# Score banks of the cross-attention in turns, hidden units rounded by ScalarE, and the self-attention's output weights rounded by ScalarE

## The chip, the cores and the metric

One NeuronCore of one Trainium2 chip runs the whole kernel in one launch. The metric is the device time of one execution in microseconds (us), taken as the median of the runs shown. Everything is computed in float32 accuracy: each operand of a large matmul is split into a rounded part ("hi") and a rest ("lo"), and three products (hi x hi, hi x lo, lo x hi) are summed in PSUM.

## The reference, cut to what matters

```python
# layer 0: cross-attention on 64 context rows, 16 heads of 16, then an MLP
q = layernorm(x, ln1) @ Wq ; k, v = split(layernorm(ctx, ln2) @ Wkv)
x = x + softmax(q k^T * 0.25) v @ Wproj + bproj
x = x + gelu(layernorm(x, ln3) @ W1 + b1) @ W2 + b2
# layer 1: self-attention on 512 rows, 16 heads of 64
n = layernorm(x, g1)
x = x + softmax((n @ Wq1)(n @ Wk1)^T * 0.125) (n @ Wv1) @ Wo1 + bo1
# then cross-attention (Wq2, Wk2, Wv2, Wo2) and a gated MLP (Wp, Wf)
```

x is (8, 512, 256), the context (8, 64, 192), the hidden width of layer 0 is 1024, the inner width of layer 1 is 1024, and Wo1 is 1024 x 256.

## The kernel before, in words

The program has four stretches: products of the context with layer 1's weights, layer 0 (the loop called loop0), layer 1's self-attention (loop3), and layer 1's cross-attention with the gated MLP (loop4). Each engine has its own function for each stretch, with the order of its work written out by hand; the engines meet through semaphores. An engine does its instructions strictly in the written order, so a wait holds up all that stands behind it.

**Layer 0's loop** has 44 iterations. Iteration i of i = 0 to 31 computes the attention scores of one piece c = i of 128 rows (16 heads x 64 keys, so 128 x 1024 numbers in two PSUM banks). A batch b is four pieces. In one iteration of the attention part the engines do the following.

- TensorE (`pe_attention0`): it turns the first half of piece i-2 (four transposes, L778), computes the scores of piece i (six matmuls), and turns the second half of piece i-2. In the middle of an iteration stand `query(b)` in iterations i = 3, 7, ... (12 matmuls of 512 columns), the attention's `output` in odd iterations (24 matmuls of 256 columns) and its `project` in even ones (12 matmuls). A layernorm's transpose (`ln_transpose`, eight at L152) stands in even iterations, for the attention's input (kind "x", i % 4 == 2) or for the MLP's (kind "g", i % 4 == 0).
- VectorE (`dve_attention0`): the largest score of each row and head (L1008), the difference to it (L1014), the sum and reciprocal of the exponents (L1001, L1004), the rests of what was turned (L162), residual additions (L1071, L1045), the statistics of the next layernorm (L239, L243, L246) and its shift (L276).
- ScalarE (`act_attention0`): the exponent (L947, with a table load), the "hi" copies (L156), the layernorm's scale (4 x 128x256) and affine step (2 x 128x512), and the MLP's GELU (L916, with a table load).
- GpSimd (`pool_attention0`): it divides the exponents (L1098), splits the layernorm's output (L159, L165), computes 1/sqrt(variance) (L256), and adds the bias to x (L1136).

The scores of every piece lie in PSUM banks 0 and 1, as do a query's projection and a layernorm's transposes. So `scores(c)` waits until `differences(c - 1)` has read the banks (semaphore `sc0_sub`), and `query` and `ln_transpose` wait in the same way.

From iteration 10 (LAG0) on, the MLP runs beside the attention, ten iterations behind: two hidden units n = 2(i - 10) and n + 1 (of 64, each 128 x 512) per iteration. Their up-projections go to bank 4, their down-projections add up in banks 6 and 7, which are thus empty in iterations 0 to 9. A hidden unit goes from `up` (TensorE) to GELU (ScalarE, into hf1), `rounds` (the "hi" part), `rests` (VectorE, the "lo" part) and `down` (TensorE). GpSimd does `rounds` for the first 48 units (iterations 10 to 33), ScalarE for the last 16:

```python
NPOOL = 2 * (N0 + 2 - LAG0)          # L683: 48
...
if NPOOL <= n < NM:                  # L943, ScalarE
    rounds(n)
```

TensorE does `down(n - 2)` after `up(n)`, and `down(n - 1)` at the end of the iteration.

**Layer 1's self-attention** has one unit s per pair of heads and batch, 64 in all, each in four parts j. Its output weights Wo1 are eight jobs of 128 x 256 (list `g4`). A job is a DMA (L353) into one of two staging halves, a rounding to "hi", and a rest to "lo": by GpSimd for jobs 0, 3 and 6, by VectorE for the others. A half can be loaded again once the job two before it has its rest (`sp_weight`). Before, VectorE rounds and takes rests of two jobs in each part of unit 0 (`dve_weight`, L357 and L162, called at L1603 to L1605). The first use of these weights, and of the staging halves as work space, is in part 3 of unit 1.

## Time and profile before

| | |
|---|---|
| median of 3 runs | 2342.82 us (2341.16 to 2347.05) |
| the profiled execution, own time | 2332.97 us |
| its span in the profile | 2331.2 us |
| TensorE busy | 2135.2 us, 92% |
| VectorE busy | 1627.0 us, 70% |
| ScalarE busy | 1449.5 us, 62% |
| GpSimd busy | 1104.8 us, 47% |
| mean granted TensorE clock | 0.97 of full |
| layer 0's loop | 112.8 to about 600 us |
| self-attention, unit 0 / unit 1 | from 612.2 / from 634.4 us |

A row of the timeline gives the start in us from the span's start, the duration, the engine, the line (a helper's line for most copies, rests and matmuls), the operation, output and input, and in brackets how long the engine had been idle and what released it. PE is TensorE, DVE is VectorE, ACT is ScalarE, POOL is GpSimd; PS is PSUM, R and F are SBUF areas, F for float32 and R for split operands. Engine times overlap, so a busy time says nothing of the end by itself; what counts is which engine waits for which at each place.

### The profile page before, as it was taken

To read this page: it belongs to the slowest core of one execution; us is meant where nothing else is said; L and a number is where in the kernel's file an instruction comes from. 1 tells how busy PE (TensorE), PEld (TensorE's weight loads), DVE (VectorE), ACT (ScalarE), POOL (GpSimd) and SP (SyncE) were. 2 spreads that over 40 slices of the span, in tenths; PEclk is the share of its full clock that TensorE was granted. 3 is DMA by queue.
4 is the path that set the end of the run, shared out by engine and by line. 5 is a ranking of instruction groups with operands and counts; after the bars stand their busy time and mean duration, and the time that the engine had idled before them with its cause. 6 is when DMAs were issued, how large, how long until landed. Compare 5 with 4: busy or idle time off the path is not lost. (4 is left out here: it accounts for less than half of the span.)

```text
span 2331.2 us, 31301 instructions
## 1 busy us (share of the span) xinstructions
PE 2135.2 (92%) x11628; PEld 1780.3 (76%) x11628; DVE 1627.0 (70%) x2353; ACT 1449.5 (62%) x2098; POOL 1104.8 (47%) x867
## 2 busy tenths in 40 slices
PE   6867999997799999999999999999998799999998
PEld 4655778786577787777777777777876689889987
DVE  6566667664578777787777878778776866666553
ACT  5444666654477777777777777777775354545431
POOL 2145455543145444454454544545444675566432
PEclk8968999999999999999999999999999999999999
DMA  7710000011000000100001000010013411111000
GB/s 237 264 41 5 21 21 21 10 48 46 28 24 15 24 24 15 37 15 24 24 14 33 18 23 26 15 33 15 17 37 130 162 46 55 55 55 46 10 10 19
DMA packets 84280, 102.67 MB, mean 44 GB/s; under 512 B 29664, under 2 KB 61152, under 8 KB 83616
## 3 DMA queue, kind: packets, MB, share of 16 engines
q1 hardware_dynamic: 84128, 100.66, 12.9%
q8 instruction: 93, 1.52, 0.3%
q14 instruction: 59, 0.48, 0.1%
HBM read 65.50 MB, written 33.82 MB: 43 GB/s over the span
## 5 line engine op out<-in xcount | busy, mean ns | idle before, releaser
L146 PE MATMUL PS<-R 128*128 128x512 f32 (+1 forms) x2944 | 1028.6, 349 | 98.9 <-DVE R L162 55.9
L147 PE MATMUL PS<-R 128*128 128x512 f32 (+1 forms) x2944 | 999.2, 339 | 0.0
L148 PE MATMUL PS<-R 128*128 128x512 f32 (+1 forms) x2944 | 998.9, 339 | 0.0
L146 PEld LDWEIGHTS PS<-R 128*128 128x128 f32 x2944 | 567.4, 193 | 213.3 <-DVE R L162 70.2
L156 ACT ACTIVATE R<-PS 64x512 fp32r<-64x512 f32 (+4 forms) x860 | 460.3, 548 | 275.6 <-PE PS L1768 129.4
L148 PEld LDWEIGHTS PS<-R 128*128 128x128 f32 x2944 | 567.0, 193 | 61.1
L147 PEld LDWEIGHTS PS<-R 128*128 128x128 f32 x2944 | 568.3, 193 | 54.9
L162 DVE TENSOR_TENSOR R<-F,R 128x1024 fp32r<-128x1024 f32 (+2 forms) x416 | 478.6, 1156 | 44.1 <-ACT R L156 22.3
L159 POOL TENSOR_SCALAR R<-F 128x512 fp32r<-128x512 f32 (+1 forms) x343 | 294.8, 862 | 347.2 <-DVE F L1921 147.0
L1463 ACT ACTIVATE F<-PS 128x1024 f32<-128x1024 f32 x256 | 262.9, 1027 | 177.5 <-DVE R L162 122.3
L159 POOL TENSOR_SCALAR R<-R 64x512 fp32r<-64x512 f32 x128 | 143.0, 1131 | 391.4 <-ACT R L156 391.4
L1549 DVE TENSOR_REDUCE F<-PS 128x2 f32<-128x1024 f32 x256 | 301.4, 1215 | 16.2 <-PE PS L1349 16.2
L162 DVE TENSOR_TENSOR R<-PS,R 128x512 fp32r<-128x512 f32 (+3 forms) x348 | 181.4, 542 | 187.5 <-ACT R L156 187.1
L165 POOL TENSOR_TENSOR R<-F,R 128x512 fp32r<-128x512 f32 (+2 forms) x126 | 233.7, 1857 | 35.7 <-ACT R L156 19.1
L1530 DVE TENSOR_TENSOR R<-PS,R 64x512 fp32r<-64x512 f32 x128 | 88.0, 688 | 221.9 <-ACT R L156 221.9
L156 ACT ACTIVATE R<-F 128x1024 fp32r<-128x1024 f32 (+2 forms) x190 | 167.0, 896 | 55.5 <-PE PS L148 54.1
L156 ACT ACTIVATE F<-PS 64x512 f32<-64x512 f32 (+3 forms) x280 | 160.1, 593 | 44.6 <-PE PS L148 37.8
L1349 PE MATMUL PS<-R 128*128 128x512 f32 x512 | 164.2, 402 | 8.6 <-ACT F L156 4.9
L1315 PE MATMUL PS<-R 128*128 128x512 f32 x512 | 163.1, 400 | 7.9 <-ACT R L156 7.3
L1311 PE MATMUL PS<-R 128*128 128x512 f32 x512 | 166.7, 407 | 1.9 <-ACT F L1463 1.9
L152 PE MATMUL PS<-F 128*128 128x128 f32 x592 | 89.6, 289 | 54.0 <-DVE F L1549 30.0
L1659 POOL TENSOR_TENSOR F<-F 128x512 f32<-128x512 f32 x64 | 83.4, 1302 | 116.0 <-DMA F<-sd 116.0
(90 smaller groups left out, 1983.5 us busy)
## 6 DMA issues: line engine op xcount, KB each, us to landing
F<-sd SPq DMA_DIRECT2D x128, 128.0 KB, 2.8
xs<-F SPq DMA_DIRECT2D x16, 512.0 KB, 2.6
F<-xs SPq DMA_DIRECT2D x16, 512.0 KB, 3.6
gd<-F SPq DMA_DIRECT2D x8, 768.0 KB, 3.5
vd<-F SPq DMA_DIRECT2D x8, 768.0 KB, 5.7
R<-gd SPq DMA_DIRECT2D x6, 1024.0 KB, 5.6
R<-vd SPq DMA_DIRECT2D x6, 1024.0 KB, 5.6
F<-in_x SPq DMA_DIRECT2D x8, 512.0 KB, 4.9
```

The source lines that it names most:

```text
L146: nc.tensor.matmul(o, L[0], Rr[0], start=start, stop=False, skip_group_check=share)
L147: nc.tensor.matmul(o, L[0], Rr[1], start=False, stop=False, skip_group_check=share)
L148: return nc.tensor.matmul(o, L[1], Rr[0], start=False, stop=stop, skip_group_check=share)
L156: return nc.scalar.activation(o, i, ACT.Identity, **k)
L159: return nc.gpsimd.tensor_scalar(o, i, 1.0, 1.0, ALU.mult, ALU.mult)
L162: return nc.vector.tensor_tensor(o, i, f32(hi), ALU.subtract)
L165: return nc.gpsimd.tensor_tensor(o, i, f32(hi), ALU.subtract)
L1311: nc.tensor.matmul(bank(h), ka[i][h][:, kk], qa[i][h], start=True, stop=False)
L1315: m = nc.tensor.matmul(bank(h), kb[i][h][:, kk], qb[i][h], start=False, stop=True)
L1349: m = nc.tensor.matmul(bank(b0 + h), qa[i][h][:, 128 * q:128 * q + 128], ka[i][h], start=True, stop=True)
L1463: nc.scalar.activation(pst3[n % 2], bank(0, 2), ACT.Exp, scale=0.125).then_inc(e3.sem, 1)
L1549: nc.vector.tensor_reduce(M3[:, q, 0:128:64], bank(b0, 2).rearrange("p (a b) -> p a b", a=2), AX.X, ALU.max).then_inc(b3_max.sem, 1)
```

## The change

It has three parts.

1. In iterations 0 to 9 of layer 0's loop, odd pieces have their scores in banks 6 and 7, even ones in banks 0 and 1. `scores(c)` then waits for `differences(c - 2)`. The layernorms' transposes of these iterations (i = 2, 6, 8) go to banks 6 and 7 and wait for `differences(i - 1)` in place of `differences(i)`. `query(1)` and `query(2)`, in banks 0 and 1, wait for the differences of pieces 2 and 6 in place of 3 and 7.
2. `rounds` is done by ScalarE for all 64 hidden units. GpSimd's 48 go away. The two events become one.
3. Wo1's jobs are rounded by ScalarE: one job in each part of unit 0 (jobs 0 to 3), and two in each of the parts 0 and 1 of unit 1 (jobs 4 to 7). The rests stay with the engines that had them, at the new places. SyncE's loads follow: job i + 2 is asked for where job i is handled.

```diff
@@ -679,9 +679,7 @@
         av0_mm, o0_hi, o0_lo = event("d_mm", 2 * NB), event("o_hi", 2 * NB), event("o_lo", 2 * NB)
         o0_mm, o0_add = event("o_mm", 2 * NB), event("x_add", 2 * NB)
         up_mm, gelu, h_lo, down_mm = [event(n, NM) for n in ("up_mm", "gelu", "h_lo", "down_mm")]
-
-        NPOOL = 2 * (N0 + 2 - LAG0)
-        h_hi, h_act = event("h_hi", NPOOL), event("h_act", NM - NPOOL)
+        h_hi = event("h_hi", NM)
         res = event("res", 2 * NB)
 
 
@@ -696,6 +694,14 @@
         norm0_at = {"x": (0, P_LN1W, P_LN1B), "g": (0, P_LN3W, P_LN3B), "s": (2, P_G1, P_B1)}
 
         turn_bank = (2, 5)
+
+        def score_bank(c):
+
+            return 6 if c < LAG0 and c % 2 == 1 else 0
+
+        def norm0_bank(i):
+            return 6 if i < LAG0 else 0
+
         first1 = (N0 + 7, N0 + 8, N0 + 9, N0 + 11)
 
         def norm0_to(kind, b):
@@ -755,7 +761,7 @@
             def query(b):
                 pe.wait_ge(ln_nl, number0["x", b])
                 wait_weights(pe, "q")
-                pe.wait_ge(sc0_sub, 4 * b - 1)
+                pe.wait_ge(sc0_sub, 4 * b - 2 if 4 * b - 1 < LAG0 else 4 * b - 1)
                 for g in range(2):
                     for k in range(2):
                         m = mm3(bank(g), [v[:, k, 128 * g:128 * g + 128] for v in W0q], [v[:, k, :] for v in ns[b % 2]],
@@ -782,11 +788,11 @@
                 b, q = divmod(c, 4)
                 pe.wait_ge(q0_lo, 2 * b + 1)
                 pe.wait_ge(k0_in[b % 2], b // 2)
-                pe.wait_ge(sc0_sub, c - 1)
+                pe.wait_ge(sc0_sub, c - 2 if c <= LAG0 else c - 1)
                 if c - 1 in norm0:
                     pe.wait_ge(ln_aff, 2 * norm0[c - 1][2] + 1)
                 for g in range(2):
-                    m = mm3(bank(g), [v[:, g, 128 * q:128 * q + 128] for v in Q1], [kd_b[b % 2][:, hl, g, :] for hl in range(2)],
+                    m = mm3(bank(score_bank(c) + g), [v[:, g, 128 * q:128 * q + 128] for v in Q1], [kd_b[b % 2][:, hl, g, :] for hl in range(2)],
                             True, True)
                 m.then_inc(sc0_mm.sem, 1)
 
@@ -863,8 +869,8 @@
                 if i % 2 == 0 and ok((i - 4) // 2, 2 * NB):
                     project((i - 4) // 2)
                 if i in norm0:
-                    pe.wait_ge(sc0_sub, min(i, N0 - 1))
-                    ln_transpose(norm0[i][2], 0)
+                    pe.wait_ge(sc0_sub, i - 1 if i < LAG0 else min(i, N0 - 1))
+                    ln_transpose(norm0[i][2], norm0_bank(i))
                 if ok(n + 1, NM):
                     up(n + 1)
                 if i % 4 == 2 and ok((i - 2) // 4, NB) and i > 2:
@@ -919,7 +925,7 @@
             def rounds(n):
                 act.wait_ge(gelu, n)
                 act.wait_ge(down_mm, n - 3)
-                act_copy(h1[n % 3][0], hf1[n % 3]).then_inc(h_act.sem, 1)
+                act_copy(h1[n % 3][0], hf1[n % 3]).then_inc(h_hi.sem, 1)
 
             act.wait_ge(g5_mm, 15)
             for job in g1:
@@ -940,7 +946,7 @@
                     act_weight(job)
                 if ok(n, NM):
                     gelus(n)
-                if NPOOL <= n < NM:
+                if ok(n, NM):
                     rounds(n)
                 if ok(i, N0):
                     act.wait_ge(sc0_sub, i)
@@ -949,13 +955,13 @@
                     query(i // 4 + 1)
                 if i in norm0:
                     kind, b, k = norm0[i]
-                    ln_affine(k, norm0_at[kind][1], norm0_at[kind][2], 0)
+                    ln_affine(k, norm0_at[kind][1], norm0_at[kind][2], norm0_bank(i))
                 if i + 1 in norm0:
                     kind, b, k = norm0[i + 1]
                     ln_scale_act(k, xbuf(norm0_at[kind][0], b))
                 if ok(n + 1, NM):
                     gelus(n + 1)
-                if NPOOL <= n < NM:
+                if ok(n + 1, NM):
                     rounds(n + 1)
                 if i % 2 == 1 and ok((i - 3) // 2, 2 * NB):
                     m_ = (i - 3) // 2
@@ -1005,20 +1011,17 @@
 
             def largest(c):
                 dve.wait_ge(sc0_mm, c)
-                nc.vector.tensor_reduce(mx4, heads(bank(0, 2)), AX.X, ALU.max).then_inc(sc0_max.sem, 1)
+                nc.vector.tensor_reduce(mx4, heads(bank(score_bank(c), 2)), AX.X, ALU.max).then_inc(sc0_max.sem, 1)
 
             def differences(c):
                 dve.wait_ge(sc0_max, c)
                 dve.wait_ge(w_lo_pool, [j.rest for j in g1 if j.by_pool][-1])
                 dve.wait_ge(t0_mm, 2 * (c - 3) + 1)
-                nc.vector.tensor_tensor(heads(E1[c % 3]), heads(bank(0, 2)), mx4.unsqueeze(2).to_broadcast([128, 16, 64]),
+                nc.vector.tensor_tensor(heads(E1[c % 3]), heads(bank(score_bank(c), 2)), mx4.unsqueeze(2).to_broadcast([128, 16, 64]),
                                         ALU.subtract).then_inc(sc0_sub.sem, 1)
 
             def rests(n):
-                if n < NPOOL:
-                    dve.wait_ge(h_hi, n)
-                else:
-                    dve.wait_ge(h_act, n - NPOOL)
+                dve.wait_ge(h_hi, n)
                 dve_rest(h1[n % 3][1], hf1[n % 3], h1[n % 3][0]).then_inc(h_lo.sem, 1)
 
             for job in g1:
@@ -1087,11 +1090,6 @@
                     next(ahead)
 
         def pool_attention0(ahead):
-            def rounds(n):
-                pool.wait_ge(gelu, n)
-                pool.wait_ge(down_mm, n - 3)
-                pool_copy(h1[n % 3][0], hf1[n % 3]).then_inc(h_hi.sem, 1)
-
             def divided(c):
                 pool.wait_ge(rec0, c)
                 ev = E1[c % 3].rearrange("p (h s) -> p h s", h=16)
@@ -1116,12 +1114,8 @@
                     divided(i - 1)
                 for job in weights0_at(i):
                     pool_weight(job)
-                if ok(n, NPOOL):
-                    rounds(n)
                 if LAG0 <= i - 1 < N0:
                     divided(i - 1)
-                if ok(n + 1, NPOOL):
-                    rounds(n + 1)
                 if i in norm0:
                     kind, b, k = norm0[i]
                     if kind == "g":
@@ -1249,6 +1243,12 @@
 
         def v3_bank(u):
             return 6 if u else 5
+
+        def weights3_at(s, j):
+
+            if s == 0:
+                return g4[j:j + 1]
+            return g4[2 * j + 4:2 * j + 6] if s == 1 and j < 2 else []
 
         def sp_attention1():
             sp.wait_ge(x_out[x_at(0, 7)], store_no[0, 7])
@@ -1276,9 +1276,8 @@
                     e = s - 3
                     if j == 1 and ok(e, N3) and e % 8 == 7:
                         sp_store(2, e // 8, xs, o3_add, e)
-                    if s == 0:
-                        sp_weight(g4, 2 * j + 2)
-                        sp_weight(g4, 2 * j + 3)
+                    for job in weights3_at(s, j):
+                        sp_weight(g4, g4.index(job) + 2)
                     at = tail3(s, j)
                     if at == 0:
                         sp.wait_ge(qk_mm, 2 * N3 - 1)
@@ -1491,6 +1490,8 @@
                         project_k(u)
                     if ok(u, N3) and u > 0 and j == 1:
                         value(u)
+                    for job in weights3_at(s, j):
+                        act_weight(job)
                     if ok(t, N3) and j in (1, 2):
                         rounded(t, j)
                     if ok(d, N3) and j == 3:
@@ -1600,9 +1601,8 @@
                             rests(4 * s + 2)
                     if ok(u, N3) and j in (1, 2):
                         largest(u, 2 * j - 2, 2)
-                    if s == 0:
-                        for job in g4[2 * j:2 * j + 2]:
-                            dve_weight(job)
+                    for job in weights3_at(s, j):
+                        dve_weight_rest(job)
                     for _ in range(early4.get(tail3(s, j), 0)):
                         next(ahead)
                     if more and j == 3 and p == 4:
@@ -1666,9 +1666,8 @@
                         pool.wait_ge(e3, 4 * t + j)
                         pool.wait_ge(d3_mm, 4 * (t - 1) + j)
                         pool_copy(P3[0][:, j, :], pst3[j % 2]).then_inc(p3_pool.sem, 1)
-                    if s == 0:
-                        for job in g4[2 * j:2 * j + 2]:
-                            pool_weight(job)
+                    for job in weights3_at(s, j):
+                        pool_weight(job)
                     for _ in range(early4_pool.get(tail3(s, j), 0)):
                         next(ahead)
                     if j == 2 and more and p == 6:
```

Three places show how the instructions of the engines move. The first is TensorE in iterations 1 and 2 of layer 0's loop: the second half of the scores of piece 0, the scores of piece 1 (six matmuls), the four transposes of piece 0 (waiting for `p_mul`, GpSimd's division), and the first matmul of the scores of piece 2. Before:

```order
L147 MATMUL PS<-R,R1 128x512
L148 MATMUL PS<-R,R1 128x512
L146 MATMUL PS<-R,R1 128x512 [waits sc_sub]
L147 MATMUL PS<-R,R1 128x512
L148 MATMUL PS<-R,R1 128x512
L146 MATMUL PS<-R,R1 128x512
L147 MATMUL PS<-R,R1 128x512
L148 MATMUL PS<-R,R1 128x512
L778 MATMUL PS<-F,F1 128x128 [waits p_mul]
L778 MATMUL PS<-F,F1 128x128 x3
L146 MATMUL PS<-R,R1 128x512 [waits sc_sub]
```

And now:

```order
L147 MATMUL PS<-R,R1 128x512
L148 MATMUL PS<-R,R1 128x512
L146 MATMUL PS<-R,R1 128x512
L147 MATMUL PS<-R,R1 128x512
L148 MATMUL PS<-R,R1 128x512
L146 MATMUL PS<-R,R1 128x512
L147 MATMUL PS<-R,R1 128x512
L148 MATMUL PS<-R,R1 128x512
L784 MATMUL PS<-F,F1 128x128 [waits p_mul]
L784 MATMUL PS<-F,F1 128x128 x3
L146 MATMUL PS<-R,R1 128x512 [waits sc_sub]
```

The order is the same; piece 1 has no wait for VectorE any more.

The second place is ScalarE in layer 0's loop where the MLP runs beside the attention: from the GELU of the second unit of an odd iteration on, over the whole of the following even one (i % 4 == 0). R1<-F1 128x512 is a rounding. Before:

```order
L916 ACTIVATE F<-PS,F 128x512 [waits up_mm]
L156 ACTIVATE R<-PS 128x512 [waits o_mm,d_mm]
L156 ACTIVATE R<-PS 128x4x128 [waits t_mm] x2
L916 ACTIVATE F<-PS,F 128x512 [waits h_lo,up_mm]
L947 ACT_TABLE_LOAD
L947 ACTIVATE F<-F 128x1024 [waits sc_sub]
L156 ACTIVATE F<-PS,F 128x512 [waits ln_tr]
L156 ACTIVATE F<-PS,F 128x512
L916 ACT_TABLE_LOAD [waits h_lo]
L916 ACTIVATE F<-PS,F 128x512 [waits up_mm]
```

And now:

```order
L922 ACTIVATE F1<-PS,F 128x512 [waits up_mm]
L156 ACTIVATE R1<-F1 128x512 [waits down_mm,gelu]
L156 ACTIVATE R1<-PS 128x512 [waits o_mm,d_mm]
L156 ACTIVATE R1<-PS 128x4x128 [waits t_mm] x2
L922 ACTIVATE F1<-PS,F 128x512 [waits h_lo,up_mm]
L156 ACTIVATE R1<-F1 128x512 [waits down_mm,gelu]
L953 ACT_TABLE_LOAD
L953 ACTIVATE F1<-F1 128x1024 [waits sc_sub]
L156 ACTIVATE F<-PS,F 128x512 [waits ln_tr]
L156 ACTIVATE F<-PS,F 128x512
L922 ACT_TABLE_LOAD [waits h_lo]
L922 ACTIVATE F1<-PS,F 128x512 [waits up_mm]
```

One rounding stands ahead of the exponent and its table load, the other ahead of the attention output's copy and of the two turned halves. The number of table loads is the same, 96 in the program.

The third place is ScalarE in the first parts of unit 1 of the self-attention, now; before, the four rows R<-F3 128x256 weren't there:

```order
L1462 ACTIVATE F3<-PS 128x1024 [waits p_lo,c_mm]
L156 ACTIVATE R3<-PS 64x512 x2
L156 ACTIVATE R3<-PS 64x512 [waits qk_mm]
L156 ACTIVATE R3<-PS 64x512
L156 ACTIVATE R<-F3 128x256 [waits w_in0]
L156 ACTIVATE R<-F3 128x256 [waits w_in1]
L1462 ACTIVATE F3<-PS 128x1024 [waits p_lo,c_mm]
L156 ACTIVATE R3<-PS 128x4x64 [waits v_set,v_mm]
L156 ACTIVATE R3<-PS 128x4x64
L156 ACTIVATE R<-F3 128x256 [waits w_in0]
L156 ACTIVATE R<-F3 128x256 [waits w_in1]
L156 ACTIVATE R3<-F3 128x1024 [waits d_mm,exp]
```

Jobs 4 and 5 stand ahead of the exponent of part 1 (L1463 before), jobs 6 and 7 behind the value's copies and ahead of the rounding of the exponents of part 1. Both pairs wait for their DMA (`w_in0`, `w_in1`).

## Rows read from the trace of the kernel before

**Rows 1.** Windows by stage: us, busy of PE, PEld, DVE, ACT, POOL, granted clock, DMA.
```profile
112.80:214.10 101.30, 69.75 (x328) 58.09 (x329) 65.74 (x113) 43.44 (x75) 49.13 (x35) 0.71 0.09 26
...
241.50:296.40 54.90, 49.90 (x308) 43.22 (x306) 37.48 (x65) 34.12 (x49) 27.68 (x20) 0.94 0.07 23
...
404.30:456.90 52.60, 47.09 (x308) 41.14 (x307) 37.40 (x65) 34.05 (x49) 27.68 (x20) 1.00 0.03 11
...
612.20:634.40 22.20, 13.77 (x51) 10.21 (x52) 16.82 (x26) 11.41 (x17) 5.49 (x7) 0.85 0.12 37
634.40:651.50 17.10, 16.03 (x76) 12.48 (x75) 12.70 (x14) 13.71 (x20) 4.28 (x4) 1.00 0.00 0
```

**Rows 2.** Timeline, PE, waits in iterations 2, 3, 6 and 7 of layer 0.
```profile
128.90 1.97 PE L152 MATMUL PS<-F 128*128 128x128 f32 x8 [3.33 <-DVE F L1014]
...
138.82 0.77 PE L146 MATMUL PS<-R 128*128 128x512 f32 x1 [2.63 <-DVE F L1014]
...
171.11 1.70 PE L152 MATMUL PS<-F 128*128 128x128 f32 x8 [2.54 <-DVE F L1014]
...
183.35 0.77 PE L146 MATMUL PS<-R 128*128 128x512 f32 x1 [6.36 <-DVE F L1014]
```

**Rows 3.** Timeline, DVE and ACT, iterations 3 and 7 of layer 0.
```profile
147.73 0.69 DVE L162 TENSOR_TENSOR R<-PS,R 128x512 fp32r<-128x512 f32 x1 [2.10 <-ACT R L156]
...
189.26 2.07 ACT L156 ACTIVATE F<-F 128x256 f32<-128x256 f32 x4
...
192.21 0.69 DVE L162 TENSOR_TENSOR R<-PS,R 128x512 fp32r<-128x512 f32 x1 [2.12 <-ACT R L156]
```

**Rows 4.** Timeline, PE, waits in iterations 25 to 27 of layer 0.
```profile
421.58 0.39 PE L146 MATMUL PS<-R 128*128 128x256 f32 x1 [0.64 <-DVE R L162]
428.29 0.39 PE L146 MATMUL PS<-R 128*128 128x256 f32 x1 [1.07 <-DVE R L162]
442.44 0.39 PE L146 MATMUL PS<-R 128*128 128x256 f32 x1 [2.39 <-DVE R L162]
...
445.47 0.47 PE L146 MATMUL PS<-R 128*128 128x512 f32 x1 [1.33 <-DVE F L1014]
```

**Rows 5.** Timeline, DVE, iterations 24 to 27 of layer 0.
```profile
411.51 0.17 DVE L246 TENSOR_SCALAR F<-F 128x4 f32<-128x4 f32 x1
...
417.86 0.58 DVE L276 SCALAR_TENSOR_TENSOR F<-F 128x4 f32<-128x4 f32 x1 [1.54 <-POOL F L256]
...
426.35 1.88 DVE L162 TENSOR_TENSOR R<-F,R 128x512 fp32r<-128x512 f32 x1
...
432.43 0.63 DVE L162 TENSOR_TENSOR R<-F,R 128x512 fp32r<-128x512 f32 x1
...
436.37 0.71 DVE L162 TENSOR_TENSOR R<-PS,R 64x64 fp32r<-64x64 f32 x4 [2.71 <-ACT R L156]
...
438.96 1.04 DVE L246 TENSOR_SCALAR F<-F 128x4 f32<-128x4 f32 x1
```

**Rows 6.** Timeline, POOL, iterations 25 and 26 of layer 0.
```profile
414.13 2.71 POOL L165 TENSOR_TENSOR R<-F,R 128x1024 fp32r<-128x1024 f32 x1
...
425.29 2.40 POOL L1136 TENSOR_TENSOR F<-F 128x1024 f32<-128x1024 f32 x1
...
437.58 2.40 POOL L165 TENSOR_TENSOR R<-F,R 128x1024 fp32r<-128x1024 f32 x1
```

**Rows 7.** Timeline, ACT, a GELU and ScalarE's own rounding behind it, late in layer 0.
```profile
581.65 0.69 ACT L916 ACTIVATE F<-PS,F 128x512 f32<-128x512 f32 x1
582.37 0.63 ACT L156 ACTIVATE R<-F 128x512 fp32r<-128x512 f32 x1
```

**Rows 8.** Line L357 (the roundings of Wo1) and the loads of Wo1, L353.
```profile
L357 DVE CAST R<-F x8: 275/282/885, 616.6 to 630.4; 128x256 fp32r<-128x256 f32 x8
...
DMA to landing us min/median/max: 2.0/2.0/2.3
```

**Rows 9.** Timeline, PE, last part of unit 0 of the self-attention.
```profile
629.18 1.11 PE L152 MATMUL PS<-F 128*128 128x128 f32 x4 [3.87 <-DVE F L1549]
```

## The prediction

> **What bounds the kernel now.** I read the windows by stage first, then TensorE's waits in the timeline, then the engine that ended each. Over the whole span TensorE is busy 92%, so what can be won lies in the stretches where it stands still. The first ten iterations of layer 0's loop take 101.3 us with TensorE busy 69.8 us at a granted clock of 0.71, so much of even that is time at 1.2 GHz; no engine is full there, it is a chain that goes round [rows 1]. With the MLP beside the attention, four iterations take 52.6 us at full clock, TensorE 47.1 busy, ScalarE 34.05, VectorE 37.4, GpSimd 27.7; the same four take 54.9 us where the clock is 0.94 [rows 1]. Unit 0 of the self-attention takes 22.2 us against 17.1 for unit 1, with VectorE busy 16.8 us in it [rows 1]. The change touches these three stretches and nothing else.
>
> **Part 1, score banks in turns (iterations 0 to 9).** It adds no instruction. It takes away waits for VectorE's difference L1014: 3.33 us before the transposes of iteration 2, 2.63 before the query of iteration 3, 2.54 before the transposes of iteration 6, 6.36 before the query of iteration 7 [rows 2]. That is 14.9 us of TensorE's standstill, but it counts only as far as VectorE's own chain then moves. I follow it with the trace's durations.
>
> - Iteration 2: the transposes start 3.3 us earlier, but ScalarE still does its affine step behind the exponent of piece 2. That step starts 1.0 us earlier, and so do the scores of piece 3, GpSimd's split and the end of iteration 3's difference.
> - Iteration 3: the query needs GpSimd's split (ready about 135.0) and the transposes of piece 1, which end about 135.2. It starts there in place of 138.82, 3.6 us earlier. The query's copies, the output's 24 matmuls and the output's rest on VectorE, now at 147.73 behind 2.10 us of idle time [rows 3], all come 3.6 us earlier. Everything VectorE does in iteration 4 stands behind that rest. Gain 3.6 us.
> - Iterations 4 and 5: VectorE is never idle before its scores arrive, and iteration 5's output waits for VectorE's rest of a turned half. Gain 0.
> - Iteration 6: the transposes no longer wait, but `value(1)` behind them needs the residual addition, and ScalarE the exponent. The value copies and VectorE's rests of them come 0.65 us earlier.
> - Iteration 7: the query can start at 177.3 in place of 183.35 [rows 2]. What then comes last is ScalarE: the exponent of piece 7, two query copies, the four layernorm scales of 2.07 us, and only then the output's copy. VectorE's rest of it moves from 192.21 [rows 3] to about 187.55. That is 4.66 us, of which 0.65 was counted: 4.0.
> - Iterations 8 and 9: ScalarE's affine step is in order behind the exponent. Gain 0.1.
>
> Sum 8.35 us. The bounds are 0, if ScalarE's and VectorE's order holds all of it back, and 14.9 us, the waits themselves. I take 8.4: the one number comes from following both queues.
>
> **Part 2, ScalarE rounds all hidden units (iterations 10 to 33).** 48 roundings leave GpSimd and come to ScalarE. There one lasts 0.63 us and starts 0.72 us behind the GELU's start [rows 7]; with the overlap that is lost before it I count 0.67 us in its queue, 5.4 us per four iterations, so ScalarE goes from 34.05 to about 39.4 of 52.6 us. No table load is added. TensorE waits four times in four iterations: 0.64, 1.07, 2.39 and 1.33 us [rows 4].
>
> - Iteration 25, 0.64 us. VectorE was late because its layernorm shift waited 1.54 us for GpSimd's L256 [rows 5], which stood behind the split L165 of 2.71 us [rows 6], which stood behind the second rounding. Without it the split starts at 410.4 in place of 412.4, L256 ends about 414.9, and VectorE's difference comes 1.8 us earlier. The wait goes.
> - Iteration 26, 1.07 us. VectorE's rest of a hidden unit took 1.88 us, where its like takes 0.63 [rows 5], while GpSimd's bias addition L1136 ran (425.29 to 427.69, [rows 6]). That addition stood behind a rounding that waited for the GELU; now it follows the division and is over by about 423.6. ScalarE's rounding delays the turned half by 0.67 us, less what iteration 25 gave. The rest then ends about 426.1, when TensorE arrives (426.2). The wait goes, narrowly.
> - Iteration 27, 2.39 and 1.33 us. Here the chain runs through ScalarE: affine step, table load, GELU, and now the rounding (+0.67), then the value copies for which VectorE is already waiting 2.71 us. On VectorE the small L246 took 1.04 us, while GpSimd's split ran; the split is now earlier, and L246 alone takes 0.17 us [rows 5, 6]: -0.87. Net 0.2 us per wait chain. What is late next is the same chain.
>
> Three times 0.64, four times 1.07 (the first two such waits come at 265.6 and 320.4), six times 0.2, and 0.6 us for the last iterations, where the waits are smaller: 1.9 + 4.3 + 1.2 + 0.6 = 8.0 us. The bounds: all 5.4 us of waits in six rounds of four iterations gone (a gain of 32), or each of 48 roundings in the chain (a loss of 32). I take 8, since the rows name what ended each wait.
>
> What the lock is worth: by durations alone the rest in iteration 26 would come 0.67 us later through ScalarE and keep its 1.88 us. The rows show 1.88 against 0.63 whenever a GpSimd addition of two SBUF operands runs beside it. The Trainium skill (SBUF — State Buffer, "SBUF: two separate sides") says that a VectorE instruction with two SBUF inputs and a GpSimd one that reads SBUF take a shared port pair as an exclusive lock for the whole instruction. By that rule it matters only that they don't meet, and the 4.3 us come; if the stretching had another cause, part 2 would give 8.0 - 4.3 = 3.7 us.
>
> **Part 3, Wo1's roundings.** VectorE loses eight of 0.28 to 0.5 us, 2.7 us in all [rows 8], and the rests of jobs 4, 5 and 7, 2.4 us, leave unit 0. ScalarE gains eight, estimated at 0.36 us, between VectorE's 0.28 and the 0.63 of twice the columns on ScalarE [rows 7, 8]. In unit 0 VectorE is the chain, but in part 0 its next work waits for ScalarE's value copies, so 0.95 us comes there, 0.3 in part 1 and 1.6 in parts 2 and 3: the transposes that wait 3.87 us at 629.18 [rows 9] come 2.85 us earlier. Unit 1 pays. Job 6 can be loaded only when VectorE has job 4's rest, now at about 640.3 (on the old scale); the DMA takes 2.0 us [rows 8], so ScalarE stands at job 6 until about 642.4, and the rounding of part 1's exponents, the exponent of part 2 and job 7 stand behind it. That rounding comes 3.1 us later; behind it VectorE has its own work (three more rests) and ends 1.1 us later. Net 2.85 - 1.1 = 1.75, I take 1.7. Bounds: +2.85, and -3.1 if unit 0 gives nothing and the stall isn't absorbed.
>
> **Sum:** 8.4 + 8.0 + 1.7 = 18.1 us. The span becomes 2331.2 - 18.1 = 2313.1, that execution's time 2332.97 - 18.1 = 2314.9. The profiled execution was 9.85 us below the median of the runs shown, so on their scale I forecast 2342.8 - 18.1 = 2324.7, say **2325 us**.
>
> **Rivals.**
>
> - *The banks bring nothing.* TensorE's queries come earlier, but ScalarE's order (exponent, query copies, scales) and VectorE's hold the chain. For it: those engines also idle only for one another in iterations 4 and 5. Against it: iteration 3's output has nothing of ScalarE's before it but two copies. Time 2325 + 8.4 = 2333. The Trainium skill (TensorE: Matmul & The Clock Gate, "HAM oscillation") tells of a kernel where double-buffering PSUM "gave no further gain"; that would be this rival. Rows 2 show the wait that it removes here, so I hold it less likely.
> - *The clock adds to it.* Four iterations take 2.3 us less at full clock than at 0.94 [rows 1], and the first ten iterations ran at 0.71, where 69.75 busy us would be 20 fewer at full clock, most of them off the chain. With fewer standstills three rounds (6.9 us) and an estimated tenth of those 20 could be won: 2325 - 9, about 2316.
> - *Wo1 loses.* The stall at job 6 isn't absorbed and unit 0 gives nothing: 2325 + 1.7 + 3.1 = 2330.
> - *ScalarE becomes the chain; slower.* Place: the second rounding of each iteration, ahead of the attention output's copy, the turned halves and the value copies. It decides if ScalarE's idle time at these places is less than the 1.3 us that an iteration adds. Then 48 x 0.67 = 32.2 us are on the path, part 2's 8.0 fall away, and 10.1 remain: 2342.8 + 32.2 - 10.1 = 2365. With one of two roundings on the path it is 2342.8 + 16.1 - 10.1 = 2349. Against it: ScalarE idles (52.6 - 34.05) / 4 = 4.6 us per iteration. For it: VectorE waits for ScalarE in iteration 27 already.
>
> **How the numbers follow.** My forecast has 0.50, the clock's case 0.20, the banks' 0.12, Wo1's 0.10, ScalarE's 0.08 (0.05 of it at 2349 or above). 0.3% is 7 us, about what a measurement of this kernel tells from no change: faster is below 2335.8. Faster: the forecast, the clock and Wo1 (0.80) less 0.04 for a smaller gain than worked out, and half of 0.12, whose time lies 3 us from the border: 0.82. Slower 0.05, same 0.13. The range reaches from 2311, the clock's case with the banks' upper bound half reached, to 2337, the banks' case with Wo1's loss: 2311 to 2337.
>
> **What would show it.** Right: the first ten iterations take about 93 us in place of 101.3; TensorE has no wait for VectorE's difference before the queries of iterations 3 and 7; four iterations with the MLP take 50.5 us at full clock, the waits of 0.64 and 1.07 are gone and one of about 2.2 is left; unit 0 takes 19.4 us and unit 1 18.2, with a ScalarE wait for a DMA. Wrong: a wait of TensorE for rests longer than 2.4 us, or VectorE idle for ScalarE over more than before in iterations 10 to 33.

## The result, and the profile after

The changed kernel takes 2314.57 us (median of 4 runs, 2312.75 to 2317.42), the kernel before beside it 2341.99 us. The ratio is 0.988, 95% interval [0.986, 0.990]. Run once more in a later comparison it gave 2317.71 us and 0.989 [0.987, 0.991], against 2339.53 for the kernel before beside it. The forecast was 2325: the time lies in its range, but the gain is 27.4 us the first time and 21.8 the second, where 18.1 were summed.

Page of the profile after, busy time of each engine:

```profile
PE 2127.5 (92%) x11628; PEld 1774.7 (77%) x11628; DVE 1610.2 (70%) x2345; ACT 1482.0 (64%) x2154; POOL 1070.6 (46%) x819
```

ScalarE has 32.5 us more than before (48 roundings of 0.63 and the output weights), GpSimd 34.2 less, VectorE 16.8 less, and TensorE 7.7 less for the same 11628 matmuls. Some 5 to 6 of these 7.7 lie in the first ten iterations (69.75 us busy before; 64.79 after, 63.49 from the first mark on), where the granted clock went from 0.71 to 0.83.

Windows by stage after, the stretches of [rows 1] (us, busy of PE, PEld, DVE, ACT, POOL, granted clock, DMA): ten iterations (from 1.3 us ahead of the first mark on; from the mark they are 89.6 us), four iterations twice, unit 0, unit 1.

```profile
117.70:208.60 90.90, 64.79 (x339) 53.72 (x338) 66.01 (x112) 42.82 (x76) 49.20 (x35) 0.83 0.10 29
235.40:285.70 50.30, 46.76 (x307) 41.34 (x307) 34.15 (x65) 39.19 (x56) 22.45 (x12) 1.00 0.07 25
336.10:388.40 52.30, 49.56 (x307) 43.50 (x306) 34.19 (x65) 39.14 (x56) 22.45 (x12) 0.93 0.07 23
593.10:612.10 19.00, 13.25 (x48) 10.16 (x49) 11.84 (x14) 12.62 (x22) 4.80 (x6) 0.82 0.10 28
612.10:631.30 19.20, 17.22 (x78) 12.90 (x78) 14.98 (x18) 15.03 (x25) 4.71 (x5) 1.00 0.05 14
```

I cut every trace at the same marks: VectorE's maximum of each piece of scores (the first of them is called the first mark), and in the self-attention the start of a unit's first exponent on ScalarE. All times in us; "rounds" are the four times four iterations from piece 12 on, "last" is pieces 28 to 31.

| | 0 to 10 | 10 to 12 | rounds | last | unit 0 | unit 1 |
|---|---|---|---|---|---|---|
| before | 101.3 | 27.5 | 54.9, 54.8, 53.1, 52.7 | 33.3 | 22.2 | 17.2 |
| after | 89.6 | 26.8 | 50.3, 50.3, 52.4, 50.3 | 34.5 | 19.0 | 19.2 |
| after, again | 89.2 | 27.1 | 52.4, 50.4, 50.7, 52.4 | 34.5 | 19.0 | 19.3 |

The profiled spans differ by only 20.2 us (2331.2 and 2311.0). Six of the missing us lie ahead of the first mark, in code that the change doesn't touch: it came at 112.8 us before and at 119.0 after, and in the twelve other traces at 115.1 to 120.1. From that mark to unit 2 the two traces differ by 26.5 us, close to the medians' 27.4; the second trace of the changed kernel differs by 22.9, with 21.8 between its medians. Of the 26.5 us, 2.0 lie between piece 31 and unit 0, where the kernels with that stretch unchanged scatter by as much (119.9 to 121.9 us).

TensorE after, from the timeline: around the query of iteration 3, where [rows 2] had 2.63 us of waiting, and the two waits that are left in a round, where [rows 4] had four.

```profile
140.69 0.48 PE L784 MATMUL PS<-F 128*128 128x128 f32 x2
141.13 0.50 PE L146 MATMUL PS<-R 128*128 128x512 f32 x1
141.46 0.39 PE L147 MATMUL PS<-R 128*128 128x512 f32 x1
141.69 0.40 PE L148 MATMUL PS<-R 128*128 128x512 f32 x1
...
143.99 0.29 PE L146 MATMUL PS<-R 128*128 128x256 f32 x1
...
424.79 0.39 PE L146 MATMUL PS<-R 128*128 128x256 f32 x1 [2.19 <-DVE R L162]
427.81 0.47 PE L146 MATMUL PS<-R 128*128 128x512 f32 x1 [1.33 <-DVE F L1020]
```

The query starts 22.1 us behind the first mark in place of 26.0, with no wait. From its second matmul on they follow each other at 0.23 us. In the kernel before, same view and query, they came at 0.43; the last row is the first matmul of the output behind it:

```profile
139.39 0.63 PE L147 MATMUL PS<-R 128*128 128x512 f32 x1
139.82 0.63 PE L148 MATMUL PS<-R 128*128 128x512 f32 x1
...
144.08 0.32 PE L146 MATMUL PS<-R 128*128 128x256 f32 x1
```

Those are the two levels of the clock, 2.4 GHz after and 1.2 GHz before. From the query's start to the output's it takes 2.86 us after and 5.26 before. ScalarE in unit 1 after, timeline: it stands for the transfer of job 6 and, shortly, of job 7.

```profile
620.46 0.42 ACT L156 ACTIVATE R<-F 128x256 fp32r<-128x256 f32 x1 [2.35 <-DMA F<-in_w_o]
621.15 1.37 ACT L156 ACTIVATE R<-F 128x256 fp32r<-128x256 f32 x2 [0.27 <-DMA F<-in_w_o]
```

### The profile page after: what moved, and what is told of

It reads as the page before. It is cut to its first block and busy times, and to the rows that moved or that the text cites. A ratio compares the mean times of both kernels' runs of the same rounds, so it can differ in the third digit from the quotient of the medians.

```text
span 2311.0 us, 31301 instructions
## 1 busy us (share of the span) xinstructions
PE 2127.5 (92%) x11628; PEld 1774.7 (77%) x11628; DVE 1610.2 (70%) x2345; ACT 1482.0 (64%) x2154; POOL 1070.6 (46%) x819
## 5 line engine op out<-in xcount | busy, mean ns | idle before, releaser
L162 DVE TENSOR_TENSOR R<-F,R 128x1024 fp32r<-128x1024 f32 (+2 forms) x416 | 465.9, 1125 | 44.0 <-ACT R L156 22.2
L159 POOL TENSOR_SCALAR R<-F 128x1024 fp32r<-128x1024 f32 (+1 forms) x295 | 265.6, 902 | 281.9 <-DVE F L1920 147.1
L156 ACT ACTIVATE R<-F 128x1024 fp32r<-128x1024 f32 (+2 forms) x246 | 200.2, 828 | 60.0 <-PE PS L148 54.8
L1096 POOL TENSOR_TENSOR F<-F 128x1024 f32<-128x1024 f32 x32 | 67.9, 2123 | 167.1 <-DVE F L1010 167.1
L1659 POOL TENSOR_TENSOR F<-F 128x512 f32<-128x512 f32 x64 | 82.6, 1290 | 120.9 <-DMA F<-sd 120.9
```

The lines of the kernel that those rows point to most:

```text
L156: return nc.scalar.activation(o, i, ACT.Identity, **k)
L159: return nc.gpsimd.tensor_scalar(o, i, 1.0, 1.0, ALU.mult, ALU.mult)
L162: return nc.vector.tensor_tensor(o, i, f32(hi), ALU.subtract)
```

## The experiments

Theory: the three parts do what the forecast worked out, and TensorE's clock adds to each, since fewer and shorter standstills leave it high for longer. Rival: the steps themselves were undersized, and the clock only went along.

### Each part alone

Each is the kernel before with one part's lines of the diff.

> The kernel before with part 1 alone (score banks in turns, with the early query and transposes); nothing else is changed. Theory A (my steps, at the clock of the trace of before): the first ten iterations take 93 us, the kernel gains 8.4 us. Theory B (the steps plus the clock: TensorE stands still less just before iteration 3's query, so that its 12 matmuls run at 2.4 GHz): the first ten iterations take 89 to 90 us, iteration 3 to 4 gains 4.8 us and not 3, the kernel gains about 12 us. Rival (the banks bring nothing by themselves): within 2 us of before. Stretches after iteration 10 as before in all of them.

> The kernel before with part 2 alone (ScalarE rounds all hidden units). First ten iterations as before, 101 us. Theory A (steps): four iterations at full clock take 50.4 us in place of 52.6, the kernel gains 8 us. Theory B (steps plus clock): the rounds that were at 0.94 take 50.4 us too, or 52.3 where the clock still falls, the kernel gains 11 to 13 us. Rival (it is only ScalarE that got longer): slower by some us, a wait for rests over 2.4 us.

> The kernel before with part 3 alone (ScalarE rounds Wo1). Theory: unit 0 takes 19.0 us in place of 22.2, unit 1 takes 19.2 in place of 17.2, with ScalarE waiting about 2.4 us for the load of job 6; net 1.2 us faster, within the noise of the timing. Rival: the stall isn't absorbed later, net slower by 1 us or more.

| | median | ratio, interval | 0 to 10 | 10 to 12 | rounds | last | unit 0 | unit 1 |
|---|---|---|---|---|---|---|---|---|
| banks | 2327.26 | 0.9945 [0.9933, 0.9957] | 89.8 | 28.4 | 55.0, 54.8, 54.7, 53.1 | 33.3 | 22.2 | 17.2 |
| rounding | 2328.59 | 0.9953 [0.9941, 0.9965] | 100.5 | 26.8 | 50.5, 52.5, 50.4, 50.6 | 34.5 | 22.2 | 17.2 |
| Wo1 | 2335.56 | 0.9987 [0.9977, 0.9996] | 100.6 | 27.5 | 54.9, 54.8, 54.7, 53.0 | 33.3 | 18.8 | 19.1 |

The kernel before in this comparison: 2339.24 us. Each part moves its own stretch; the banks alone also give back 0.9 us between pieces 10 and 12. The gains are 12.0, 10.7 and 3.7 us by the medians, 26.3 in all, beside 27.4 and 21.8 for the changed kernel: as far as the scatter lets one see, the parts add up. The banks came out as theory B said. The rounding's 10.7 lies between A's 8 and B's 11 to 13. Wo1 has 1.5 us on the marks (1.2 expected), which the interval of its ratio takes in. Where a kernel leaves the first ten iterations as they were, they take 100.5 to 101.4 us.

### The query's wait put back

```diff
 # the changed kernel, query(b)
-pe.wait_ge(sc0_sub, 4 * b - 2 if 4 * b - 1 < LAG0 else 4 * b - 1)
+pe.wait_ge(sc0_sub, 4 * b - 1)
```

> The changed kernel, but the query of a block waits again for the differences of the chunk just before it, as in the kernel before, while the scores' banks still alternate. Forecast's reading (the first wait of iterations 3 and 7, about 3.3 and the larger part of 6.4 us, is ended by the query's own wait, so that letting it go early is most of the first part's gain): ten iterations grow from 89.6 to 93 to 97 us, the kernel to 2318 to 2322 (ratio 0.990 to 0.992). Rival (the scores, whose wait was loosened as well, carry the gain and the query would be waited for little): ten iterations 90 to 91 us, within 1.5 us of the changed kernel, ratio 0.988 to 0.989.

2320.53 us, ratio 0.9934 [0.9915, 0.9953]; ten iterations 97.8 us. Timeline, TensorE, the queries of iterations 3 and 7:

```profile
142.97 0.77 PE L146 MATMUL PS<-R 128*128 128x512 f32 x1 [2.63 <-DVE F L1020]
...
185.16 0.77 PE L146 MATMUL PS<-R 128*128 128x512 f32 x1 [6.89 <-DVE F L1020]
```

The two queries' waits alone give back 8.2 of the 11.7 us that ten iterations had gained. The forecast's reading holds, and ten iterations came out even a little above its band. The other 3.5 us stay with the alternating scores and transposes.

### The clock alone

Products that nothing uses, put where TensorE stands idle ahead of these two queries. Every wait of the kernel before stays.

```diff
 # the kernel before, TensorE's loop; fill(k, b) is k matmuls of 128x512 into bank b
+if i in (3, 7):
+    fill({3: 4, 7: 12}[i], 6)
 if i % 4 == 3 and ok(i // 4 + 1, NB):
     query(i // 4 + 1)
```

> The kernel before, with products that nothing uses added on TensorE: 4 of 128x512 ahead of iteration 3's query and 12 ahead of iteration 7's, into a bank that is empty there, where TensorE idles on a wait anyway. Nothing else moves, and no wait is taken away. Theory (the first ten iterations lose time to the clock after each long wait of TensorE, and the part of the change's gain that was not forecast is this clock): the granted clock of the first ten iterations rises from 0.71 to 0.77 or more, the query of iteration 3 and what follows it runs at the short spacing, ten iterations take 98 to 100 us instead of 101.3, and the kernel 2336 to 2338 us against 2339.2 (ratio 0.998 to 0.999). Rival (the clock does not answer to such products, or the waits of the ramp swallow what it gives): ten iterations within 0.5 us of 101.3, ratio 1.000; if the added products delay the query by more than the clock gives, up to 1.0015.

2329.68 us against 2338.04, ratio 0.9963 [0.9950, 0.9976]: more work, and a faster kernel. Timeline, TensorE, the query of iteration 3, and the window of ten iterations:

```profile
141.15 0.47 PE L146 MATMUL PS<-R 128*128 128x512 f32 x1 [1.32 <-DVE F L1020]
141.46 0.40 PE L147 MATMUL PS<-R 128*128 128x512 f32 x1
```

```profile
115.10:213.00 97.90, 69.51 (x345) 57.92 (x346) 65.87 (x113) 43.59 (x75) 49.24 (x35) 0.79 0.09 27
```

The query starts at the same place, 26.04 us behind the first mark in both kernels. Its matmuls now run at full clock, from its start to the output's it takes 2.84 us in place of 5.26, and the first four iterations take 35.1 us in place of 37.5: 2.4 us from the clock alone. (In three other traces with these iterations unchanged they took 36.7 to 37.7; in one of them the query's first five matmuls came at full clock too.) The ten iterations win 3.4 us against the trace of before, 2.7 against the shortest of the others. The median won 8.4, more than the added products' own stretch shows; what lies behind the other 5 us I can't tell from one trace.

### The lock between VectorE and GpSimd

Two kernels move GpSimd's bias addition: in the kernel before it goes ahead of the second rounding; in the changed kernel it is held back until ScalarE's second rounding.

```diff
 # the kernel before, pool loop: the addition of bias to xbuf moved up
+<the addition, L1136>
 if ok(n + 1, NPOOL):
     rounds(n + 1)
-<the addition, L1136>
 # the changed kernel, ahead of the addition
+if ok(n + 1, NM) and i < N0:
+    pool.wait_ge(h_hi, n + 1)
```

> The kernel before, with GpSimd's bias addition ahead of its second rounding in odd iterations of layer 0; all roundings stay with GpSimd. Theory (the addition at the wrong moment stretches VectorE's rest in iteration 26 and its like): the rest takes 0.63 us again, TensorE's waits of 1.07 us go, those of 0.64 and 2.39 stay, 4 us faster. But the rounding now waits up to 0.7 us for the addition where the GELU is ready before it, so a little may be lost. Rival (what helps is that ScalarE rounds, not the order): rests as long as before or the second rounding late, no gain.

> The changed kernel, but in the first layer's loop GpSimd's bias addition (2.40 us) additionally waits until ScalarE has rounded the second unit of hidden products of that iteration, so that it falls again on VectorE's rest of those products. Theory (GpSimd's bias addition running beside VectorE's subtraction stretches that subtraction from 0.63 us to about 1.9, and this is what the PE waits of 0.64 and 1.07 us in a four-iteration round were made of): a rest of 1.5 to 1.9 us is back wherever the addition stands, once or twice in four iterations, the four-iteration round grows from 50.4 to 51.5 to 52.5 us, over the four rounds and the ramp 5 to 9 us in all, so 2319 to 2324 us against 2314.6 of the changed kernel (ratio to the kernel before 0.992). Rival (the gain of the second part is ScalarE's earlier rounding alone, and GpSimd's place does not matter): within 0.1% of the changed kernel, ratio to the kernel before 0.988 to 0.989, rounds still 50.4.

Addition moved up: 2330.55 us, ratio 0.9970 [0.9956, 0.9983], rounds 51.4, 51.4, 51.4 and 53.9; of the four waits of [rows 4] the one of 1.07 us is gone and 0.64 and 2.39 are as before. At full clock a round is 1.2 us shorter; the 8.7 us by the medians are twice the 4 expected, and part of it is that the clock fell in one of the four rounds, in place of three of four. Addition held back: 2306.88 us against 2338.04, rounds 51.1, 51.2, 51.2 and 51.2. Its ratio of 0.988 [0.986, 0.990] is what the rival said, not the 0.992 of the theory: the 0.8 us a round, some 3 in all, don't stand out of the scatter of a whole run, and only the marks show them. Timeline, GpSimd and VectorE, iteration 26: first the kernel with the addition moved up, then the one with it held back (there in iteration 26 too).

```profile
420.19 2.38 POOL L1127 TENSOR_TENSOR F<-F 128x1024 f32<-128x1024 f32 x1
...
423.31 0.68 DVE L162 TENSOR_TENSOR R<-F,R 128x512 fp32r<-128x512 f32 x1
```

```profile
407.32 2.40 POOL L1132 TENSOR_TENSOR F<-F 128x1024 f32<-128x1024 f32 x1 [2.10 <-ACT R L156]
...
407.76 1.29 DVE L162 TENSOR_TENSOR R<-PS,R 128x512 fp32r<-128x512 f32 x2 [4.30 <-ACT R L156]
408.96 1.31 DVE L162 TENSOR_TENSOR R<-F,R 128x512 fp32r<-128x512 f32 x1
```

The rest with two SBUF operands takes 0.68 us when the addition is over, 1.31 when it meets its last 0.8 us, and took 1.88 when it met its last 1.3 [rows 5, 6]. In both cases where they meet it ends 0.54 to 0.55 us behind the addition (410.27 and 409.72; 428.23 and 427.69), however early it started: I read that as standing until the addition was over, and then running. The two rests just ahead of it have one operand in PSUM and took 1.29 us with the addition beside them. That is the rule of the Trainium skill (SBUF — State Buffer, "SBUF: two separate sides"), and the trace agrees down to PSUM operands being free of it. I had expected 1.5 to 1.9 us and rounds of 51.5 to 52.5: ScalarE's rounding ends early enough that the two meet only at the end, so the stretch costs 0.8 us a round in place of 1.1 to 2.1. Of these, 0.42 to 0.45 us are a new wait of TensorE in iteration 26 (and its like). The rest goes with the clock, which fell for a short time in each of the four rounds. The last of them, windows (columns as above):

```profile
387.86:439.06 51.20, 48.39 (x308) 42.54 (x307) 35.58 (x66) 39.16 (x57) 22.94 (x12) 0.97 0.03 12
```

### Job 6 and 7 a part later

```diff
 # the changed kernel, weights3_at(s, j)
-return g4[2 * j + 4:2 * j + 6] if s == 1 and j < 2 else []
+return g4[4:6] if s == 1 and j == 0 else g4[6:8] if s == 1 and j == 2 else []
```

> The changed kernel, but of the four jobs of output weights that ScalarE rounds in unit 1 of the self-attention, two stand in its third part instead of its second, so that ScalarE doesn't wait for their transfer (2.35 and 0.27 us waited for DMA in the changed kernel's profile). Theory (unit 1 grew by 2.0 us because ScalarE stood waiting for the transfer with the chain's copies queued behind it): unit 1 takes 17.2 to 18.2 us instead of 19.2, the kernel 2312.8 to 2313.8 us against 2314.6 (ratio 0.9875 to 0.988). Rival (unit 1 grew by the rounding itself, 0.42 us and more a job beside VectorE's rests, wherever it stands): unit 1 19.0 to 19.4 us, the kernel as the changed one within 0.03%.

2311.42 us, ratio 0.9889 [0.9870, 0.9907]; unit 1 takes 18.5 us. Timeline, ScalarE:

```profile
616.19 1.06 ACT L156 ACTIVATE R<-F 128x1024 fp32r<-128x1024 f32 x1
619.17 1.03 ACT L1462 ACTIVATE F<-PS 128x1024 f32<-128x1024 f32 x1 [1.91 <-DVE R L162]
620.09 1.67 ACT L156 ACTIVATE R<-F 128x256 fp32r<-128x256 f32 x3
```

No wait for DMA is left, and that gives back 0.64 us of the 2.0 by which unit 1 had grown: short of the expectation, above the rival's. The other 1.3 us are not the transfer. No run separates the roundings on ScalarE from the rests on VectorE, but the trace points at VectorE: the exponent above waits 1.91 us for it. Timeline, VectorE, in this kernel and then in the kernel before:

```profile
615.95 1.21 DVE L162 TENSOR_TENSOR R<-F,R 128x256 fp32r<-128x256 f32 x2
617.18 0.76 DVE L162 TENSOR_TENSOR R<-PS,R 128x256 fp32r<-128x256 f32 x2
617.86 1.22 DVE L162 TENSOR_TENSOR R<-F,R 128x1024 fp32r<-128x1024 f32 x1
...
640.17 0.76 DVE L162 TENSOR_TENSOR R<-PS,R 128x256 fp32r<-128x256 f32 x2 [0.26 <-ACT R L156]
640.84 1.22 DVE L162 TENSOR_TENSOR R<-F,R 128x1024 fp32r<-128x1024 f32 x1
```

The two rests of jobs 4 and 5 (1.21 us) stand ahead of the value's, and the rest of the exponents starts 7.5 us into the unit in place of 6.5. That is 1.0 of the 1.3 us.

### The wait that is left, and all together

The second rounding moved behind ScalarE's copies; unused products in the changed kernel's ramp; both with the later jobs; and the changed kernel again.

```diff
 # the changed kernel, ScalarE's loop
-if ok(n + 1, NM):
-    rounds(n + 1)
 <the copy of the attention output, the value copies>
+if ok(n + 1, NM):
+    rounds(n + 1)
 # TensorE's loop, ahead of scores(i) and ahead of output(...)
+if i in (3, 9):
+    fill(8, 4)
+if i in (5, 9):
+    fill(10, 4)
```

> The changed kernel, with products that nothing uses added on TensorE where it idles in the ramp: 8 of 128x512 ahead of the scores of iterations 3 and 9, 10 ahead of the output of iterations 5 and 9, into a bank that is empty there. Theory (even in the changed kernel the ramp loses to the clock: granted 0.83 over the first ten iterations, where the waits of 3 to 5 us stand): the clock of the ramp rises to 0.88 or more, ten iterations 87 to 89 us instead of 89.6, the kernel 1 to 2.5 us under the changed kernel of the same call (ratio between them 0.999 to 0.9995). Rival (the added products delay what stands behind them by more than the clock gives): ten iterations 90 to 92 us, the kernel 0.5 to 3 us over the changed one.

> The changed kernel, but ScalarE's second rounding of hidden products in an iteration (0.63 us) stands behind its copy of the attention output and the copies of value products instead of ahead of them. Theory (the one wait of about 2.2 us that each four-iteration round keeps, on VectorE's rest of the attention output, comes a rounding later than it need, and falls at full clock): the wait shrinks to 1.5 to 1.7 us, the four-iteration rounds take 49.7 to 50.2 us instead of 50.4, the kernel 1 to 3 us under the changed kernel of the same call. Rival (the rounding moved back makes the rest of the hidden products late, and the wait goes from one place to the other): rounds 50.3 to 51.5 us, the kernel within 0.1% or up to 3 us over the changed one.

> The changed kernel with three edits together: the added products of the ramp, ScalarE's second rounding behind its copies, and two of the output-weight jobs of unit 1 a part later. If each gives by itself what its theory says (1 to 2.5 us, 1 to 3 us, 0.6 us as run alone), the sum is 2.5 to 6 us under the changed kernel of the same call, and it beats both kernels. If the added products or the moved rounding delay what stands behind them, 0 to 5 us over it.

> The changed kernel once more, for comparison with the others of this call. Forecast: ratio to the kernel before 0.9875 to 0.989, as first measured (0.9882); ten iterations 89.4 to 89.8 us, of the four rounds one or two 52 to 52.6 and the others 50.3 to 50.5, unit 0 18.8 to 19.0, unit 1 19.1 to 19.3 us. Should the start of the loop, in code that the change doesn't touch, again lie anywhere from 113 to 120 us, the scatter of single runs is from there and from behind unit 2, and not from the places that the change touches.

| | median | ratio, interval | 0 to 10 | rounds | last | unit 1 |
|---|---|---|---|---|---|---|
| changed, again | 2317.71 | 0.9893 [0.9874, 0.9913] | 89.2 | 52.4, 50.4, 50.7, 52.4 | 34.5 | 19.3 |
| filled | 2312.49 | 0.9871 [0.9850, 0.9893] | 88.8 | 50.4, 50.4, 50.7, 52.5 | 34.5 | 19.1 |
| rounding late | 2307.97 | 0.9858 [0.9838, 0.9878] | 89.2 | 49.4, 49.4, 49.4, 49.4 | 33.8 | 19.3 |
| all three | 2299.94 | 0.9825 [0.9806, 0.9844] | 88.8 | 49.4, 49.4, 49.4, 49.4 | 33.8 | 18.5 |

The kernel before beside these: 2339.53 us. All three together beat both kernels. The gains are larger than expected throughout: against the changed kernel of this comparison (the control) 5.2 us for the fill (1 to 2.5 expected; the two intervals overlap), 9.7 for the late rounding (1 to 3) and 17.8 for all three (2.5 to 6). Timeline, TensorE, the same two waits of a round with the rounding late:

```profile
419.07 0.39 PE L146 MATMUL PS<-R 128*128 128x256 f32 x1 [1.50 <-DVE R L162]
422.10 0.47 PE L146 MATMUL PS<-R 128*128 128x512 f32 x1 [1.33 <-DVE F L1020]
```

The wait of 2.19 has lost 0.69 us, the rounding and its overhead, and a round at full clock 0.9. So at this one place the forecast's slower rival was real: ScalarE's rounding stood on the chain. What the other 0.2 us of a round are is open. And in eight rounds of two kernels (this one and all three together) no clock fell, where it fell in 32 of the 48 rounds of the twelve other traces. Where it falls is seen in the changed kernel's round of 52.4 us, windows (columns as above):

```profile
358.30:365.00 6.70, 6.65 (x46) 5.51 (x45) 5.51 (x8) 6.11 (x7) 2.21 (x2) 1.00 0.00 0
365.00:372.40 7.40, 5.27 (x32) 4.34 (x32) 5.06 (x18) 5.38 (x12) 4.44 (x4) 1.00 0.01 2
372.40:377.00 4.60, 4.04 (x16) 3.48 (x17) 4.57 (x7) 1.61 (x2) 0.19 (x1) 0.56 0.60 215
377.00:382.00 5.00, 5.00 (x25) 4.26 (x24) 1.66 (x3) 2.09 (x5) 4.38 (x2) 0.72 0.15 38
```

TensorE waits 2.16 us up to 372.43, and right behind that it is granted 0.56. In the kernel before and in the changed one's second trace too, every fall in the rounds lies in the fourth iteration, behind this wait. A fall costs a round 2.1 us where its mean clock is 0.93 (52.4 less 50.3), and 0.1 to 0.4 where it is 0.97 (50.4 to 50.7).

The filled ramp has a higher clock (0.90 against 0.81 in its ten iterations), yet wins only 0.4 us there against the control: the waits there are ended by the other three engines, and I read it as a TensorE whose faster stretches mostly end in a wait. That reading is not tested. Windows, the filled kernel and the control (the changed kernel again):

```profile
119.30:208.10 88.80, 67.30 (x373) 55.95 (x371) 65.95 (x112) 42.91 (x76) 49.27 (x35) 0.90 0.10 29
119.70:208.90 89.20, 63.75 (x325) 52.77 (x324) 65.64 (x112) 41.70 (x75) 49.19 (x35) 0.81 0.10 29
```

For all three the marks give 0.4 + 8.3 + 0.6 + 0.7 = 10 us against the control, and the medians 17.8. In the traces 3.4 of the rest lie between the last piece and unit 0, and 5 behind unit 2. The edits don't touch the second; the first still has the moved rounding in it, but with the rounding late alone it takes 120.3 us, against 120.9 in the control. Those stretches scatter by as much between all the traces (117.5 to 121.9 us, and 1674 to 1684). Why the medians differ by more than the marks stays open.

## Why the prediction was right, and where it was short

- **Part 1, forecast 8.4, measured 11.5** on ten iterations with the banks alone (0.9 of it given back up to piece 12; 12.0 by the medians). The step on iteration 3 was right: the query comes 3.9 us earlier (3.6 forecast). The step's words "the output's rest on VectorE, all come 3.6 us earlier" failed: by piece 4 the gain is 6.3 us, because the query's twelve matmuls ran at 2.4 GHz in place of 1.2, which is 2.4 us (2.86 us in place of 5.26), as much as the filled kernel before won there. The output behind them ran at 2.4 GHz before as well. The sum was made with the trace's durations, and the query's was one at 1.2 GHz.
- **Part 2, forecast 8.0, measured 10.7.** A round at full clock went from 52.7 to 50.3 us (50.5 forecast), the waits of 0.64 and 1.07 are gone and one of 2.19 is left, as written; the lock's wait of 1.07 us a round is shown by moving the addition alone, which takes it away and a round from 52.7 to 51.4. The forecast counts three waits of 0.64 us where the four rounds had four. The four rounds sum to 215.4 us before, and to 203.4 and 205.8 in the two traces after. At full-clock lengths the gain would be 9.4; the first trace has 2.6 more, the second nearly nothing. Over all traces the clock fell in 14 of the 16 rounds of the four kernels with the old waits (the kernel before, banks, Wo1, filled before), and in 13 of the 24 of the six with the waits of the changed kernel; their sums are 216.4 and 204.1 us on average, so about 3 us more than the 9.4. The last three iterations cost 1.1 us that the forecast had as a gain of 0.6. One sign that the forecast gave for being wrong did come, with a kernel that was faster all the same: VectorE's idle time for ScalarE from piece 12 to 28 rose from 58.1 us to 65.1. It is a poor sign by itself, since VectorE was also busy 3.2 us less in a round (37.4 and 34.2 in the windows); but with the rounding late it is 58.9, so part of it was ScalarE's rounding on the chain.
- **Part 3, forecast 1.7, measured 1.5** on the marks with Wo1 alone (unit 0 -3.3, unit 1 +1.9; forecast -2.85 and +1.1), 1.2 in the changed kernel, and 0.9987 [0.9977, 0.9996] on the whole. The stall for job 6 came as worked out, 2.35 us, but only 0.64 us of unit 1's growth was its price; most of the rest lies, by the trace, with VectorE's rests of jobs 4 and 5. The term of unit 1 is the one that was too small, 1.1 us for a measured 1.9.
- **The step that was short is the sum**: it kept the clock out, as a rival with a chance of 0.20. Its argument from [rows 1] was right, and it was not an alternative to the forecast but a term of it. That its 9 us are what was missing (27.4 less 18.1) is luck: the second measurement misses 3.7, and the shares are others. It had 6.9 us from three rounds without a fall and 2 from the first ten iterations; the runs show 2.4 in the ten iterations by the query alone, and about 3 in the rounds on average. The rest of the 9.3 is steps of the rounds sized a little low, and scatter. So the theory and its rival at the head of the experiments both hold in part.
- **The range**: its low end of 2311 is not what its words give; 2316 less half of the 6.5 us up to the banks' bound is 2313. The time lies above both.
- **The banks' rival** is refuted: it is the largest part. The Trainium skill (TensorE: Matmul & The Clock Gate, "HAM oscillation") says of another kernel that double-buffering PSUM "gave no further gain". Here it gave 0.55% [0.43%, 0.67%], since the bank's wait was the last to end ahead of two queries.
- **The scale**: adding 9.85 us to bring the profiled execution to the median was right for the kernel before. Its trace began its loop 2 to 7 us earlier than any other.

## What to carry to other kernels

When a change takes standstills of TensorE away, look at the spacing of the matmuls behind each: as far as they run at 1.2 GHz, up to half of their time can be won beside the wait (here 2.4 us beside 3.9), and it belongs in the sum. Where one instruction's duration varies two- or threefold in a trace, look for the GpSimd instruction beside it before moving anything else; changing the order of one addition gave a round 1.2 us. A stall that is plain in a trace may still cost a quarter of its length (0.64 of 2.62 us), while 0.7 us off the one wait behind which the clock falls was worth 0.9 us a round and the falls as well.

## What the runs showed that was not expected

- Adding 16 unused matmuls made the kernel before faster by 0.37% [0.24%, 0.50%].
- The clock fell in 32 of 48 rounds whose longest wait was 2.2 to 2.4 us, always at the end of that wait or within 1.5 us behind it, and in none of 8 rounds where it was 1.5. One kernel doesn't tell the odds: with the addition moved up it fell in one round of four, with the addition held back in all four.
- The start of the first loop, behind code that is the same in all kernels, lies anywhere from 112.8 to 120.1 us, so one trace's span misjudges a change of this size by a quarter.
